# Dropping unchosen blocks by adding -1e30 in PSUM ahead of the gelu, with a new merge order, in a fused decoder layer

## The reference, cut to what matters

```python
prob = softmax(xf @ Wr.T + br)                    # 16 blocks
_, idx = top_k(prob, 4)
mask = zeros((n, 16)).at[arange(n)[:, None], idx].set(1.0)
h = einsum('nf,ibf->nib', xf, W1.reshape(16, 64, 256))
h = gelu(h, approximate=False) * mask[:, :, None]
y = einsum('nib,fib->nf', h, W2.reshape(256, 16, 64))
```

## Time and profile before

| | |
|---|---|
| median of 3 runs | 414.06 us (413.67 to 414.71) |
| the profiled execution | 413.82 us, its span in the trace 412.1 us |
| PE, DVE, ACT, POOL busy, share of the span | 93%, 77%, 60%, 37% |
| granted TensorE clock, mean | 0.998 of full |

### The profile page before, as it was taken

How to read it: one execution, slowest core, us unless ns; L and a number is a source line. 1 busy time by engine, 2 the same in 40 slices (tenths; PEclk the granted TensorE clock), 3 DMA queues, 4 the chain that set the end, 5 groups by cost and what they waited for, 6 DMA issues and landing times.

```text
span 412.1 us, 9281 instructions
## 1 busy us (share of the span) xinstructions
PE 381.5 (93%) x3144; PEld 327.1 (79%) x3144; DVE 315.3 (77%) x924; ACT 246.8 (60%) x528; POOL 151.4 (37%) x173
## 2 busy tenths in 40 slices
PE   3889899999999989998999999999999989899895
PEld 3768769888899868687898778989869877668794
DVE  4998798367676868888887788688778888777653
ACT  5355642536638894476789356678974256994240
POOL 6488545738645123453422325231113320000101
PEclk9999999999999999999999999999999999999999
DMA  7993435553255313242241612220123000000000
GB/s 224 328 372 107 149 102 150 196 171 92 70 173 162 97 28 77 63 118 78 77 130 41 166 32 46 79 78 25 29 78 104 1 2 14 14 3 2 13 14 27
DMA packets 21134, 38.45 MB, mean 93 GB/s; under 512 B 2528, under 2 KB 11616, under 8 KB 21088
## 3 DMA queue, kind: packets, MB, share of 16 engines
q1 hardware_dynamic: 20272, 37.06, 29.6%
q10 hardware_dynamic: 816, 0.79, 0.6%
HBM read 25.52 MB, written 5.24 MB: 75 GB/s over the span
## 4 chain that ended last, share of the span: by engine, by line
PE 64%; DVE 17%; issue 7%; ACT 6%; POOL 3%; DMA 2%; SPq 0%; DVEq 0%; POOLq 0%; ACTq 0%
PE bank L452 12%; PE acc L539 8%; PE bank L625 6%; PE bank L692 5%; PE bank L677 5%; PE bank L483 5%; PE bank L506 4%; PE bank L614 3%; ACT xs L831 3%; PE bank L565 3%; PE bank L637 2%; PE bank L520 2%; PE bank L491 2%; PE bank L509 2%; DVE wqkv_lo L918 2%
## 5 line engine op out<-in xcount | busy, mean ns | idle before, releaser
L831 ACT ACTIVATE xs<-xs,xneg 128x256 f32<-128x256 f32 x128 | 54.3, 500 | 13.4 <-DVE xneg L1089 13.1
L1248 POOL TENSOR_TENSOR a_lo<-a_flat,a_hi 128x512 fp32r<-128x512 f32 x32 | 41.9, 1311 | 30.2 <-ACT a_flat L752 30.2
L452 PE MATMUL bank<-x_hi,wqkv_hi 128*128 128x256 f32 x144 | 45.6, 317 | 7.3 <-DVE wqkv_lo L918 7.3
L1237 POOL TENSOR_TENSOR q_T<-q_T,rope_s 128x512 f32<-128x512 f32 x24 | 31.1, 1301 | 54.7 <-DMA rope_s<-rope_t 54.4
L539 PE MATMUL acc<-wo_s,a_hi 128*128 128x256 f32 x256 | 50.1, 294 | 1.1 <-POOL a_lo L1248 1.1
L1266 POOL TENSOR_TENSOR rstd<-var_eps,half 128x1 f32<-128x1 f32 x24 | 13.2, 551 | 99.2 <-DVE var_eps L976 99.2
L1089 DVE CUSTOM_DVE_ANT_0 xs<-bank,mask_s 128x256 f32<-128x256 f32 x128 | 46.1, 419 | 1.7 <-PE bank L614 1.6
L506 PE MATMUL bank<-v_s,p_near 128*128 128x129 f32 x256 | 41.6, 277 | 1.5 <-POOL p_far L1255 1.1
L539 PEld LDWEIGHTS acc<-wo_s,a_hi 128*128 128x128 f32 x256 | 39.3, 189 | 3.3 <-POOL a_lo L1248 1.8
L452 PE MATMUL bank<-x_lo,wqkv_hi 128*128 128x256 f32 x144 | 41.3, 287 | 0.0
L452 PE MATMUL bank<-x_hi,wqkv_lo 128*128 128x256 f32 x144 | 41.1, 285 | 0.0
(11 more groups left out here) (152 smaller groups left out, 954.2 us busy)
## 6 DMA issues: line engine op xcount, KB each, us to landing
wo_s<-wo_parts SPq DMA_DIRECT2D x24, 512.0 KB, 3.4
rope_s<-rope_t SPq DMA_DIRECT2D x54, 128.0 KB, 2.3
wo_parts<-wo_s SPq DMA_DIRECT2D x8, 512.0 KB, 3.1
stage<-in_wqkv SPq DMA_DIRECT2D x5, 512.0 KB, 4.5
xs<-in_wo SPq DMA_DIRECT2D x8, 256.0 KB, 3.8
y<-in_x SPq DMA_DIRECT2D x4, 256.0 KB, 2.9
ctx_s<-in_ctxT SPq DMA_DIRECT2D x4, 256.0 KB, 3.1
mask_s<-in_mask SPq DMA_DIRECT2D x4, 256.0 KB, 2.9
```

Of the source, the lines that this page charges most:

```text
L452: ins = mm(ps, lhs[i], rhs[j], start=(k == 0 and n == 0), stop=(last and n == 2))
L831: activation(xs[:, t, m, m2, :], xs[:, t, m, m2, :], ACT.Exp, bias=xneg[:, t, m, m2:m2 + 1], scale=-1.0)\
L1237: g.tensor_tensor(dst, dst, (rope_s if b else rope_t)[:, n % 2], ALU.add).then_inc(sig["rotated", 0], 1)
L1248: g.tensor_tensor(a_lo[:, j % 2], a_flat[:, j % 2], a_hi[:, j % 2].bitcast(F32), ALU.subtract)\
```

## The change

The mask product no longer has a bank of its own. PE adds it to the W1 product in the same bank (`start` is set on the first matmul of the bank alone), and what it adds is 0 for a chosen block and -1e30 for another, since `keep` now holds `(marked >= 0) * -1e30` in place of `marked < 0`. The gelu of such a value is zero, so DVE's product behind the gelu is gone (16 instructions of 128x512), the signal `masked` with it, and `ffn` waits for the gelu itself. `hidden` takes one place of the ring and not two. `ORDER` is another string of the same letters: no operation is added or taken away by it.

```diff
+DROP = -1.0e30
-         "outproj": 1, "turn_z": 1, "route": 1, "turn_m": 1, "hidden": 2, "ffn": 1, "turn_w": 2}
+         "outproj": 1, "turn_z": 1, "route": 1, "turn_m": 1, "hidden": 1, "ffn": 1, "turn_w": 2}
 ORDER = (
-    "rrrrrrrmmrsrrssmmrrmsrmmssrmmrsmmmmmmscsmmmmcsmmmrmcmmssmmrrcccmmmmmrrsmmmmmcmssmrrcmmmmmrmmmssmsmrrrmccy"
+    "rrrrrrmmrrrsssmrmrmmsmmrsssmrmmrmmmmssrrmmmmmmssscmmmmmmrcmcmmmmrrmmmmmcmmrrccmmmmmcssssrrmmmmxssmsrrrccc"
...
-                "hidden": ("gelu" if k == 0 else "masked", i), "ffn": ("ln3", 0),
+                "hidden": ("gelu", i), "ffn": ("ln3", 0),
...
                 ps = claim("hidden", b, part, t, 0)
                 for m in range(n):
                     for k in range(CK):
-                        ins = mm(ps[:, m * P:(m + 1) * P], w1_s[:, k, (n * part + m) * P:(n * part + m + 1) * P],
-                                 z_T[:, t, k, :], start=(k == 0), stop=(k == CK - 1))
-                ins.then_inc(filled, 1)
-                ps = claim("hidden", b, part, t, 1)
+                        mm(ps[:, m * P:(m + 1) * P], w1_s[:, k, (n * part + m) * P:(n * part + m + 1) * P],
+                           z_T[:, t, k, :], start=(m == 0 and k == 0), stop=False, skip_group_check=True)
                 wait_for(pe, "mask_T", b, 0, t)
                 for m in range(n):
                     ins = mm(ps[:, m * P:(m + 1) * P], pick_s[:, n * part + m, :], keep_T[:, t * P:(t + 1) * P],
-                             start=True, stop=True)
+                             start=False, stop=True, skip_group_check=True)
                 ins.then_inc(filled, 1)
...
-                        wait_for(pe, "masked", b, n * HPARTS // HT, t)
+                        wait_for(pe, "gelu", b, n * HPARTS // HT, t)
...
-                do(v.tensor_scalar(keep[:, t, 0:NBLK], marked[:, t, :], 0.0, None, ALU.is_lt))
-
-            def hidden(b, part, t):
-                n = HT // HPARTS
-                g = g_T[:, t, n * part:n * (part + 1), :].rearrange("p h n -> p (h n)")
-                wait_for(dve, "gelu", b, part, t)
-                wait_filled(dve, "hidden", b, part, t, 1)
-                v.tensor_tensor(g, g, bank("hidden", b, part, t, 1)[:], ALU.mult).then_inc(sig["masked", t], 1)
+                do(v.tensor_scalar(keep[:, t, 0:NBLK], marked[:, t, :], 0.0, DROP, ALU.is_ge, ALU.mult))
```

More of the change, by code:

```diff
@@ L131 @@
          "turn_k": 1, "turn_q": 1, "xscore": 2, "turn_p": 1, "xmix": 1, "turn_o": 1, "turn_ox": 1,
-         "outproj": 1, "turn_z": 1, "route": 1, "turn_m": 1, "hidden": 2, "ffn": 1, "turn_w": 2}
+         "outproj": 1, "turn_z": 1, "route": 1, "turn_m": 1, "hidden": 1, "ffn": 1, "turn_w": 2}
 ORDER = (
-    "rrrrrrrmmrsrrssmmrrmsrmmssrmmrsmmmmmmscsmmmmcsmmmrmcmmssmmrrcccmmmmmrrsmmmmmcmssmrrcmmmmmrmmmssmsmrrrmccy"
[L137 to L140, removed]
+    "rrrrrrmmrrrsssmrmrmmsmmrsssmrmmrmmmmssrrmmmmmmssscmmmmmmrcmcmmmmrrmmmmmcmmrrccmmmmmcssssrrmmmmxssmsrrrccc"
+    "mmmmmmsssymmmmyxsxysmmxmmmrymxxmmyxmmxmryyyxxxrrxmmmmxxxrxxsxxymmmysmsmxyyyyyxyxmsryyyrxyyyxmmmxsmmysrcxc"
+    "mmmmxxccsssmmryymccmxmyrxsmmmsxysmmxxymmmxmmyxxxymmxmmxxyoxxyyrrmyyyryyxxyynxyxyrnyxxrxyyymmmmyxsssxyysxm"
+    "oyccmmxnnxxsscccrynyxcroxoymmmmmxyymsssmmmmyxxoynnyxxxyyooxxyyyxxymxxrxyyymyxxxryyxxmxyyynxymsyyxxssoymmm"
+    "mymmymmxnmxmoymmmycmcmmmmxnccnooyxccxyynxyxyoyxyxynoyyyxxxyyyxxxxnyyxyyxxyyxxyxyxxnoyxyxnxnxooyyxnnoynoon"
     "onnoooon")
@@ L174 @@
             "probs_T_odd": QUADS, "xout": QUADS, "xattn": 2, "o_T": 1, "z_T": 1, "route": 7,
-            "route_exp": 1, "mask_T": 1, "gelu": HPARTS, "masked": HPARTS, "stored": 16}
+            "route_exp": 1, "mask_T": 1, "gelu": HPARTS, "stored": 16}
 def build_decoder(nc, x, xT, ctxT, mask, wqkv, wo, wkvT, xwq, xwo, xbias, wrT, br, w1T, w2T,
@@ L848, in hidden @@
                 n = HT // HPARTS
-                wait_filled(act, "hidden", b, part, t, 0)
+                wait_filled(act, "hidden", b, part, t)
                 activation(g_T[:, t, n * part:n * (part + 1), :].rearrange("p h n -> p (h n)"),
-                           bank("hidden", b, part, t, 0)[:], ACT.Gelu).then_inc(sig["gelu", t], 1)
+                           bank("hidden", b, part, t)[:], ACT.Gelu).then_inc(sig["gelu", t], 1)
             for kind, b, i, t in plan:
@@ L885, in _ @@
                 elif kind == "turn_z":
-                    wait_filled(act, "hidden", b - 1, HPARTS - 1, t, 0)
+                    wait_filled(act, "hidden", b - 1, HPARTS - 1, t)
                     evacuate(z_T[:, t].rearrange("p k q -> p (k q)"), bank(kind, b, 0, t)[:, 0:CK * P], kind, b, 0, t, "z_T")
@@ L890, in _ @@
                 elif kind == "turn_m":
-                    wait_filled(act, "hidden", b - 1, HPARTS - 1, t, 1)
+                    wait_filled(act, "hidden", b - 1, HPARTS - 1, t)
                     evacuate(keep_T[:, t * P:(t + 1) * P], bank(kind, b, 0, t)[:].bitcast(BF16)[:, 0:P],
@@ L1199, in _ @@
                     router(b, t)
-                elif kind == "hidden":
-                    hidden(b, i, t)
                 elif kind == "ffn":
```

## The result

The kernel after takes 399.87 us (398.11 to 402.77, 4 runs) where the one before takes 414.38 (413.67 to 415.51): ratio 0.9654, interval 0.9592 to 0.9716. That is 14.5 us of gain and not 4.6 to 5.0.

A forecast was written before the change was run, and what follows sets the result against it. PE was taken as the bound, busy 93%, with 30.6 us idle to win. Named gains of 5.7 us less 1.1 for new waits gave -4.6 us: 409.2 profiled, 409.4 as median, range 403.5 to 414.3.

The forecast's parts named there:

- the order's share of the sum: New order string: waits spread out at 187.11, 148.01, 296.12, 372.26 and in the head; 0.9, 0.8, 0.5, 0.9 and 1.0 us.
- the masking product's: DVE's 16 removed products: 1.0 us gained at PE's wait at 333.43, 0.6 at the scaling at 386.00, 0 at the end.
- the charge of 1.1: Loss for waits the new order may open elsewhere: between 0 and 5.7 us, taken as 1.1, about a fifth.
- the head's 1.0: Near 1 and far 0 ahead of rot 4: 1.9 us lost, 1.14, 1.2 and 0.6 won, net -1.0 us.
- three named waits: PE's waits at 187.11 (query split), 148.01 (exp) and 296.12 (ACT copy), shortened by 0.9, 0.8 and 0.5 us.
- PE's own work: The 64 mask products as additions stay at 219 ns each and the gelu keeps its time: 0 us, bound 1.9 better.
- The end: Last masking product, 401.09 to 401.78, is hidden behind PE's W2 products: gain 0; 0.7 us if that cover were gone.
- the gain of 0.6 through the scaling: At 386.00, without the product, the scaling of batch 3's output projection, then norm, router and `keep`, come 0.6 us earlier.
- The wait of 0.88 at 372.26: Mask transpose of tile 1 waits for the router; moved behind both halves of tile 0's hidden products, gaining 0.9 us.
- The waits only move: Rival: the charge for new waits is 5.7 us, not 1.1, and time stays at 413.9; chance 0.17.
- The ring gets air: Rival: fewer ring places and a freer DVE queue also shorten unnamed waits, 5.0 us more, 404.4; chance 0.18.
- Score bursts block ACT: Rival: six near, near, far rows block ACT 3.7 us each, costing PE 6.8 us, 416.1; chance 0.13.

The follow-up runs named there:

- e1: The kernel after with the old order string, so the new arithmetic alone: 413.81 us, ratio 0.9978.
- e11: New arithmetic, with the new order up to operation 418 and the old order from there on: 402.9 us, ratio 0.9724.
- i1: The kernel before (old arithmetic), with the new order up to operation 418 and the old order from there on: 408.2 us, ratio 0.9851.
- e2: The kernel before (old arithmetic, masking product on DVE) with the whole new order string: 418.91 us, ratio 1.0115.
- h1: The kernel after with its first 118 operations in the old order: 401.38 us, ratio 0.9676.
- i2: The kernel before (old arithmetic), with the old order up to operation 418 and the new tail: 424.7 us, ratio 1.026.
- e3: The kernel after, with each hidden product claiming a second, unused place of the ring that the gelu frees: 399.28 us, ratio 0.9639.
- e7: The kernel after with score steps near 1 and far 0 put back behind rotation step 4: 403.43 us, ratio 0.9742.
- i4: New arithmetic, with the old order up to operation 131 and the new order behind it: 406.05 us, ratio 0.9805.

## Why the prediction was right or wrong

**The failed step** is the order's share of the sum, which was too small, and its separation from the arithmetic. Of the 4.6 us forecast, 1.6 were the masking product's (1.0 at 333.43 and 0.6 at 386.00), and 4.1 less the charge of 1.1, so 3.0, the order's. Measured one after the other, the arithmetic gives 0.6 to 1.1 (`e1`) and the order, with the new arithmetic in place, 13.9. Of these, 10.9 lie ahead of operation 419 (`e11`), where the sum had the head's 1.0 and 2.2 for three named waits, less the charge; and 3.0 to 3.4 in the tail, where it had 0.9.

**The charge of 1.1 for new waits** was not the trouble by itself: such waits did open, 1.6 us of them in 47 to 110 us (idle 2.4 instead of 0.75, of which 1.24 at 84.55 for POOL's sum of `q_T`). What failed is that nothing stood against it. Of the 6.9 us of idle time in 110 to 310 us I took 2.2, the three waits of the earlier trace rows, and let the unnamed ones stay; 6.7 went, small pieces included. About 4 of these are the order's own (`i1`), and PE's busy time fell by 3.0 besides. So the sum of new waits and lost ones has the other sign.

**Arithmetic and order** were priced apart, each against the waits of the old trace, and added. DVE's product was costed where PE already waited for it or just behind it, which under the old order is all it is worth. What it forbade was not priced: a `hidden` straight ahead of a quantisation for which PE's next transpose waits. The new order makes use of this at the two quantisations of batch 3's output and in batch 1's network, and with the product it would have cost 4 us (`e2`) instead of giving 13.9. The trace of before had 7.3 us of DVE waiting for the gelu, and I read it as idle time of an engine that is not the bound. Idle time costs nothing where nothing that PE needs is queued behind it; here it was a place in an in-order queue.

**The head**, -1.0 forecast, is -1.5 by `h1`, not clear of the spread of the runs. The parts were right in the main: the stall, 2.19 us ending at 22.24, was forecast as 2 to 3 (its place as 17 to 20 and its releaser as `rope_t`; the weights came late in this run, and POOL's sum of that table is named), the waits of 1.14 at 27.88 and 1.2 for the quantised weights are gone. PE's row there:

```profile
19.03 1.02 PE L484 MATMUL bank<-q_T,k_T 128*128 128x512 f32 x2
22.24 1.78 PE L484 MATMUL bank<-q_T,k_T 128*128 128x512 f32 x2 [2.19 <-POOL q_T L1227]
23.81 1.91 PE L492 MATMUL bank<-q_T,k_T 128*128 128x512 f32 x2
```

What was not seen is that the clock is at half behind the stall (0.64, then 0.50): `near` 1 takes 1.78 us where `near` 0 took 1.02, and `far` 0 1.91.

**PE's own work.** The mask products as additions take what they took the earlier trace rows, the gelu too, by line and form in the kernel after:

```profile
L849 ACT ACTIVATE stage<-bank 128x512 f32<-128x512 f32 x16 | 9.6, 597 | 11.3 <-PE bank L682 11.0 <-PE bank L668 0.2
...
L682 PE MATMUL bank<-keep_T,pick_s 128*128 128x128 bf16 x64 | 6.2, 219 | 0.0
```

The price of 0 was right for both. PE's busy time was forecast the same within 1 us and is 3.0 less. This is the order's (`e1` has 381.4), and 2.1 of it are one group, the transposes of `turn_p`: 37.7 us before (line 625), 35.6 after (line 626), with 256 instructions in both. Busy time has short gaps of the pipeline in it, so this may be waiting that the idle time doesn't show; that was not tested. **The end** at 0 was right. `keep` in the last batch still costs PE 0.85 us, 0.79 before; the gain of 0.6 through the scaling shows as 0.6 us by which the kernel after draws further ahead from its last projection (385.56 us before, 375.04 after) to the transpose of this `keep` (391.52 and 380.39). The wait of 0.88 at 372.26 is gone, as forecast.

**DVE busy** was forecast at 304 and is 294.4. The products had 10.8; the other 10 are the order's: `e2` with all its products has 304.5.

**The rivals.** "The waits only move" had the time of the arithmetic alone, 413.9 against 413.8, and its argument was the Trainium skill's (Perfetto Trace Analysis, Identifying Performance Opportunities): improve the most contended engine. Under the old order the trace agrees, 0.6 us. Under the new one it does not: a wait on the second engine, with no work in it, is worth 13.4 us to the first. The Trainium skill (PSUM — Partial Sum Buffer, Engine vs sequencer instructions) says that VectorE's queue is strictly first in, first out; the rows of `i2` show it, and this was the rule to price. "The ring gets air" had the nearest time of the cases, 404.4, but was wrong in its cause as to the ring (`e3`: 0.6 us less, not more), and half right in DVE's queue. "Score bursts block ACT" fell: the waits of PE for ACT that the trace of the kernel after lists, 0.8 us the longest, all lie at 330.12 us or later, and the last product of the scores starts at 297.26.

**Left open**: why some runs with the same gaps have less of the low clock than others, which waits the 3 us of the tail under the new arithmetic come from, and what the other 1.7 of the 3.5 us of `e7` are.

## What to carry to other kernels

Where an edit takes a wait out of an in-order queue, look at what stands behind the waiting instruction and what a new order may put there; the old trace prices only what the old order exposed. If a change has an edit and a new order, think of four kernels and not of two terms, and run the two mixed ones first. When orders are joined for an experiment, read the trace at the seam before the difference: here two of the joins made waits of 2.9 us of their own.

## What the hardware showed

A gap of PE can cost more than its length. After 2 us with 0.05 us of work the granted clock was 0.64 in the next 2 us and 0.50 in the 2 after them (20 to 26 us of the kernel after); in the three stretches of `h1` there, PE busy for 5.57 of 6 us, it stayed at 1.00. It also stayed at 1.00 behind a gap of 1.16 us in `e7`, and fell to half behind gaps of 2.31 and 2.89 us (`i2`), 2.92 (`i4`) and 3.38 (`e7`).

The time of a DVE operation between two SBUF operands goes with what GpSimd does beside it. In the kernel before, the same split of a query took 0.77 us in one place and 1.65 in another:

```profile
115.72 1.65 DVE L1077 TENSOR_TENSOR parts<-q_tmp,parts 128x512 fp32r<-128x512 f32 x1
...
186.19 0.77 DVE L1077 TENSOR_TENSOR parts<-q_tmp,parts 128x512 fp32r<-128x512 f32 x1
```

GpSimd was in a sum from 115.27 to 116.82 and in the next from 116.78 beside the first, and in nothing but the end of a causal mask, up to 186.43, beside the second. The Trainium skill (SBUF — State Buffer, SBUF: two separate sides) has the rule: a DVE operation with two inputs in SBUF and a GpSimd operation that reads SBUF share a port pair, and one of them holds it for a whole instruction. The trace agrees roughly: the end of the sum at 116.82 and the 0.69 us of this split at its shortest would make 117.5, and it ended at 117.37. The means of the kernels before and after differ, 944 ns against 832 for this line, but that is 0.8 us of DVE time only. That the order's 10 us of DVE time come from this is possible, and was not tested.
